# Product matmuls between the main matmuls of a two-layer graph kernel, one unit later

## The chip, the cores and the metric

The kernel runs on one core of one Trainium2 chip. The metric is the device time of one execution in microseconds (us). Engines: PE (TensorE) multiplies; PEld is PE's loading of stationary operands, which the trace records apart; DVE is VectorE, ACT ScalarE, POOL GpSimd, SP SyncE, which here issues DMAs.

## The reference

```python
def _L0_gnn_ref(h, adj, W_neigh, b_neigh, W_self, b_self):
    deg = jnp.sum(adj, axis=1, keepdims=True) + 1e-05
    adj_norm = adj / deg
    h_neigh = adj_norm @ h
    out = h_neigh @ W_neigh.T + b_neigh + h @ W_self.T + b_self
    return jax.nn.relu(out)

def _L1_gnn_ref(x, adj, W, b):
    rowsum = adj.sum(axis=1)
    d_inv_sqrt = jnp.where(rowsum > 0, rowsum ** (-0.5), 0.0)
    normalized_adj = d_inv_sqrt[:, None] * adj * d_inv_sqrt[None, :]
    support = normalized_adj @ x
    out = support @ W + b
    return jax.nn.relu(out)

x = _layernorm(x + _L0_gnn_ref(x, adj, ...), axis=-1)
x = _layernorm(x + _L1_gnn_ref(x, adj, ...), axis=-1)
```

x is 4096 x 256, adj 4096 x 4096, the weights are 256 x 256, all float32.

## The kernel before

**Tiles and units.** Each of the two layers goes through 8 blocks of 512 output rows. A block has 16 units (u = 0 to 15); a unit is one DMA of 128 x 1024 numbers of the transposed adj into a ring of 4 buffers `raw`. Every float32 operand is split in two parts: hi, the number rounded to the fp32r format (ACT, L256), and lo, the rest (DVE, L389). A product of two numbers is then three matmuls, hi x hi, lo x hi and hi x lo.

**Main matmuls (L675).** PE waits for `l_ready`, the lo of the unit, and issues 12 matmuls of 512 columns: 2 halves f of the features, 2 pieces q of 128 rows of adj, 3 passes each. They sum into `ps_main`, one of two PSUM buffers by the block's parity. The stationary operands are the features: `xs` in layer 0, `zs` (and the last part of `xs`) in layer 1. After a unit PE adds to `unit_done`; ACT's hi of the unit four later waits for that.

**The epilogue.** The sums of a block are finished while the next block runs: at unit 3 of their programs ACT and DVE split them into `st_hi` and `st_lo` (`stl_ready`), and PE multiplies them by the layer's weights, a product for each of the four tiles t of 128 rows: `product`, six matmuls of 256 columns in a row (L613), into `ps_epi[:, t, 0:256]`. `epilogue` places tile t behind the main matmuls of unit t + 1, and signals `tile_done`. In layer 0 eight matmuls of one column (L634) form the row sums behind unit 0, and the last tile waits until DVE has read these (`rs_copied`). DVE's program then has, in its unit 5 + t, `scale_product` (L419, waits for `tile_done`) ahead of the lo of that unit, `add_self` (L429) and `add_residual` (L436) behind it; ACT squares at its units 8 and 10 (L275), and norms and next features follow up to unit 15. DVE and ACT work through units ahead of PE, as far as the ring of four allows.

**The self product.** In layer 0 the product of x itself with `W_self` is formed in advance: `xt` is split into the same `st_hi` and `st_lo` at unit 9 (10 in the first block; `xt_unit`), after ACT has seen all four `tile_done`, and `prologue` places the six matmuls of tile t behind unit `xt_unit(b) + t` on PE, into `ps_epi[:, t, 256:512]`.

So there are 4 products in each of 15 epilogues and of 8 prologues, six matmuls each. The epilogue of the very last block has its own code (L693) and is left as it is. Every engine's program is in the order in which it is written; middle blocks run in a hardware loop.

Of the kernel before, what the change touches and what calls it, by code (L numbers as in the profile page):

```python
# [24 lines left out]
F = 256  # L25
P = 128
FH = F // P
# [3 lines left out]
TB = IB // P  # L31
UJ = 2
# [11 lines left out]
def build(nc, x_nat, xt_in, adj_in, wn_in, bn_in, ws_in, bs_in, w1_in, b1_in, out):  # L44
# [6 lines left out]
    with ctx:  # L51
        def sb(name, shape, dt=f32):
            return ctx.enter_context(nc.sbuf_tensor(name, shape, dt))

        def sem(name):
            return ctx.enter_context(nc.semaphore(name))
# [8 lines left out]
        acc = sb("acc", [P, 2, UW])  # L65
        st_hi = sb("st_hi", [P, FH, IB], f32r)
        st_lo = sb("st_lo", [P, FH, IB], f32r)
        xt = sb("xt_sb", [P, FH, IB])
        wn = sb("wn_sb", [P, 2, FH, F], f32r)
        ws = sb("ws_sb", [P, 2, FH, F], f32r)  # L70
# [6 lines left out]
        ones = sb("ones", [P, 1])  # L77
# [18 lines left out]
        ps_epi = ctx.enter_context(nc.psum_tensor("ps_epi", [P, TB, 2 * F], f32))  # L96
# [7 lines left out]
        ones_set = sem("ones_set")  # L104
        xh_ready, xl_ready = sem("xh_ready"), sem("xl_ready")
        wh_ready, wl_ready = sem("wh_ready"), sem("wl_ready")
        xth_ready, xtl_ready = sem("xth_ready"), sem("xtl_ready")
        h_ready, l_ready, acc_done = sem("h_ready"), sem("l_ready"), sem("acc_done")
        acc_folded = sem("acc_folded")
        unit_done = sem("unit_done")  # L110
        sth_ready, stl_ready = sem("sth_ready"), sem("stl_ready")
        rs_summed, rs_copied = sem("rs_summed"), sem("rs_copied")
        tile_done, tile_read = sem("tile_done"), sem("tile_read")
# [9 lines left out]
        def slot(u):  # L123
            return u % RING

        def is_last(e):

            return isinstance(e, int) and e == NB - 1

        def is_first(b):  # L130
            return isinstance(b, int) and b == 0

        def xt_unit(b):

            return 10 if is_first(b) else 9

        def x_stage(c):

            if c == 0:
                return acc[:, 1, :].rearrange("p (t f) -> p t f", t=XC)  # L140
            return (res, tt)[c % 2][:, :, :]
# [7 lines left out]
        def moving_weight(layer, part, k):  # L149
            if layer == 0:  # L150
                return wn[:, part, k, :]
            return (w1_lo if part else w1_hi)[:, k, :]

        def stationary(layer, part, jt, f):

            if layer == 0:
                return xs[:, jt, part, f * P:(f + 1) * P]
            src = zs[:, jt] if jt < ZOWN else xs[:, jt - ZOWN]
            return src[:, part, f * P:(f + 1) * P]

        def layers(eng, one_block, last_epilogue):


            for layer in range(2):
                one_block(layer, 0, 0, None if layer == 0 else (0, NB - 1))
                with eng.Fori(1, NB - 1, 2) as b:
                    one_block(layer, b, 1, (layer, b - 1))
                    one_block(layer, b + 1, 0, (layer, b))
                one_block(layer, NB - 1, 1, (layer, NB - 2))
            last_epilogue((1, NB - 1))  # L170
# [434 lines left out]

        @block.tensor
        def _(pe):
            def product(ps, rows, weight):

                passes = [(st_hi, 0), (st_hi, 1), (st_lo, 0)]  # L610
                for k in range(FH):
                    for q, (st, part) in enumerate(passes):
                        last = pe.matmul(ps, st[:, k, rows], weight(part, k),  # L613
                                         start=(k == 0 and q == 0), stop=(k == FH - 1 and q == 2))
                return last

            def prologue(b, u):

                t = u - xt_unit(b)
                if 0 <= t < TB:  # L620
                    if t == 0:
                        pe.wait_ge(wl_ready, 2)
                        pe.wait_ge(xtl_ready, b + 1)

                    product(ps_epi[:, t, F:2 * F], slice(t * P, (t + 1) * P), lambda part, k: ws[:, part, k, :])

            def epilogue(layer, e, parity, u):
                n = e + layer * NB
                if u == 0 and layer == 0:

                    pe.wait_ge(acc_folded, e + 1)
                    pe.wait_ge(ones_set, 1)
                    for t in range(TB):
                        last = pe.matmul(ps_epi[:, TB - 1, t:t + 1], acc[:, parity, t * P:(t + 1) * P],  # L634
                                         ones[:, :], start=True, stop=True)
                    last.then_inc(rs_summed, 1)
                if 1 <= u < 1 + TB:
                    t = u - 1
                    if t == 0:
                        pe.wait_ge(stl_ready, n + 1)  # L640
                    if t == TB - 1 and layer == 0:
                        pe.wait_ge(rs_copied, e + 1)

                    product(ps_epi[:, t, 0:F], slice(t * P, (t + 1) * P),
                            lambda part, k: moving_weight(layer, part, k)).then_inc(tile_done, 1)

            def one_block(layer, b, parity, epi):
                g0 = b * NU + layer * NB * NU
                ps = ps_main[parity]
                for u in range(NU):  # L650
                    if epi is None and u < WHOLE:

                        pe.wait_ge(x_first_full[u], 16)
                        pe.wait_ge(raw_full[slot(u)], 16)
                        for f, q in [(f, q) for f in range(FH) for q in range(UJ)]:
                            jt = u * UJ + q
                            last = pe.matmul(ps[:, f, :], x_stage(0)[:, jt, f * P:(f + 1) * P],  # L657
                                             raw[:, slot(u), q * IB:(q + 1) * IB], start=(jt == 0), stop=False)
                        last.then_inc(unit_done, 1)
                        continue  # L660
                    if epi is None and u % 2 == 0:
                        pe.wait_ge(xl_ready, u // 2 + 1)
                    if layer == 1 and epi[0] == 0:
                        pe.wait_ge(z_ready, UJ * (u + 1))
                    if layer == 1 and epi[0] == 1 and u == 0:
                        pe.wait_ge(wl_ready, 3)


                    pe.wait_ge(l_ready, g0 + (u + 1))
                    ends = layer == 1 and is_last(b) and u == NU - 1  # L670
                    for f, q in [(f, q) for f in range(FH) for q in range(UJ)]:
                        jt = u * UJ + q
                        cols = slice(q * IB, (q + 1) * IB)
                        for i, (part, mov) in enumerate(((0, hi), (0, lo), (1, hi))):
                            last = pe.matmul(ps[:, f, :], stationary(layer, part, jt, f), mov[:, slot(u), cols],  # L675
                                             start=(jt == 0 and i == 0), stop=(jt == JT - 1 and i == 2))
                        if ends and q == UJ - 1:
                            last.then_inc(half_done, 1)
                    if not ends:
                        last.then_inc(unit_done, 1)  # L680
                    if epi is not None:
                        epilogue(*epi, 1 - parity, u)
                    if layer == 0:
                        prologue(b, u)

            def last_epilogue(epi):
                n = 2 * NB - 1
                passes = [(st_hi, 0), (st_hi, 1), (st_lo, 0)]
                for k in range(FH):
                    pe.wait_ge(stl_ready, n + 1 + k)  # L690
                    for t in range(TB):
                        for q, (st, part) in enumerate(passes):
                            last = pe.matmul(ps_epi[:, t, 0:F], st[:, k, t * P:(t + 1) * P],  # L693
                                             moving_weight(1, part, k),
                                             start=(k == 0 and q == 0), stop=(k == FH - 1 and q == 2))
                        if k == FH - 1:
                            last.then_inc(tile_done, 1)

            layers(pe, one_block, last_epilogue)


# [33 lines left out]
```

## Time and profile before

| | us |
|---|---|
| median of 3 runs | 800.73 (800.4 to 802.11) |
| span of the profiled execution | 800.8 |
| PE busy | 782.1 (98%) |
| DVE busy | 577.4 (72%) |
| ACT busy | 386.9 (48%) |
| DMA of adj, share of 16 engines | 56.6% |

The profiled execution is within 0.1 us of the median. PE is busy all through the span; DVE is busier in layer 0 than in layer 1. Records of matmuls overlap (a matmul of 512 columns is recorded with 0.39 us while they start every 0.23 us), so the pace of PE is read from the starts, not from the busy time.

### The profile page before, as it was taken

The page shows a single profiled execution, that of the slowest core. Times are in us where ns is not written, and L with a number is a line of the kernel's source. Part 1 is how long each engine was busy: PE and PEld are TensorE (multiplying, and loading weights), DVE is VectorE, ACT ScalarE, POOL GpSimd, SP SyncE. Part 2 cuts the span into 40 slices and gives each one's busy share as a digit, 9 for nine tenths or more (in the row PEclk, how much of TensorE's full clock was granted, in tenths as well). Part 3 has the DMA queues.
Part 4 walks back from the last instruction along what each step waited for, and adds up shares of the span by engine and source line. Part 5 has one row for each costly group of instructions (what it writes and reads, how often), then busy time and mean ns, then how long its engine had stood idle before and what let it go on. Part 6 is the DMA issues. An engine that isn't in the chain of part 4 may idle for free.

```text
span 800.8 us, 11034 instructions
## 1 busy us (share of the span) xinstructions
PE 782.1 (98%) x3704; PEld 653.0 (82%) x3704; DVE 577.4 (72%) x868; ACT 386.9 (48%) x528; POOL 0.3 (0%) x6
## 2 busy tenths in 40 slices
PE   7899999999999999999999999999999999999995
PEld 4678888888888888888888888888888888888884
DVE  5799989899898998989966554555546455554643
ACT  3463745536446364454554545445444544545451
POOL 0000000000000000000000000000000000000000
PEclk9999999999999999999999999999999999999998
DMA  8767574755647556465565575746575574657540
GB/s 258 274 252 239 179 244 154 253 183 166 236 155 236 193 174 236 157 233 189 181 227 165 175 255 174 250 162 237 180 236 187 171 246 162 236 180 239 180 158 27
DMA packets 54459, 160.93 MB, mean 201 GB/s; under 512 B 5024, under 2 KB 18464, under 8 KB 54432
## 3 DMA queue, kind: packets, MB, share of 16 engines
q1 hardware_dynamic: 46224, 152.46, 56.6%
q10 hardware_dynamic: 8208, 8.13, 2.9%
q8 instruction: 15, 0.25, 0.1%
q14 instruction: 12, 0.10, 0.0%
HBM read 152.17 MB, written 8.39 MB: 201 GB/s over the span
## 4 chain that ended last, share of the span: by engine, by line
PE 94%; DMA 2%; DVE 2%; ACT 1%; issue 0%; SPq 0%
PE ps_main L675 84%; PE ps_epi L613 8%; DMA raw<-adj_t 2%; PE ps_main L657 1%; PE ps_epi L634 1%; DMA tt<-x_nat 1%; DVE lo L389 0%; DVE acc L565 0%; ACT hi L256 0%; PE ps_epi L693 0%; DVE tt L436 0%; DVE stats L585 0%; DVE tt L419 0%; DVE xs L389 0%; ACT tt L359 0%
## 5 line engine op out<-in xcount | busy, mean ns | idle before, releaser
L256 ACT ACTIVATE hi<-raw 128x1024 fp32r<-128x1024 f32 x254 | 269.4, 1061 | 352.8 <-PE ps_main L675 327.8
L389 DVE TENSOR_TENSOR lo<-raw,hi 128x1024 fp32r<-128x1024 f32 x254 | 310.4, 1222 | 145.3 <-ACT hi L256 145.2
L675 PE MATMUL ps_main<-hi,xs 128*128 128x512 f32 x1136 | 366.3, 392 | 4.3 <-DVE lo L389 4.3
L675 PE MATMUL ps_main<-hi,zs 128*128 128x512 f32 x896 | 283.0, 390 | 0.0
L675 PEld LDWEIGHTS ps_main<-hi,xs 128*128 128x128 f32 x1136 | 214.2, 189 | 49.3 <-DVE lo L389 3.6
L675 PE MATMUL ps_main<-lo,xs 128*128 128x512 f32 x568 | 222.4, 392 | 0.0
L675 PEld LDWEIGHTS ps_main<-hi,zs 128*128 128x128 f32 x896 | 168.3, 188 | 34.3
L675 PE MATMUL ps_main<-lo,zs 128*128 128x512 f32 x448 | 174.7, 390 | 0.0
L565 DVE TENSOR_TENSOR acc<-acc,raw 128x1024 f32<-128x1024 f32 x112 | 136.3, 1217 | 0.0
L675 PEld LDWEIGHTS ps_main<-lo,xs 128*128 128x128 f32 x568 | 107.3, 189 | 20.0 <-issue 0.2
L675 PEld LDWEIGHTS ps_main<-lo,zs 128*128 128x128 f32 x448 | 84.2, 188 | 16.3
L419 DVE SCALAR_TENSOR_TENSOR tt<-ps_epi,d_cur,bias 128x256 f32<-128x256 f32 x32 | 15.4, 483 | 39.2 <-PE ps_epi L613 38.5
L389 DVE TENSOR_TENSOR st_lo<-ps_main,st_hi 128x1024 fp32r<-128x1024 f32 (+1 forms) x17 | 19.8, 1162 | 21.6 <-ACT st_hi L256 21.6
L281 ACT ACTIVATE tt<-tt,nmr,inv_root 128x256 f32<-128x256 f32 x60 | 32.5, 588 | 4.3 <-DVE nmr L473 4.3
L256 ACT ACTIVATE st_hi<-ps_main 128x1024 fp32r<-128x1024 f32 (+1 forms) x17 | 16.6, 978 | 33.3 <-PE ps_main L675 33.3
L275 ACT ACTIVATE ps_epi<-tt,nmean 128x256 f32<-128x256 f32 x60 | 27.5, 459 | 0.0
L436 DVE SCALAR_TENSOR_TENSOR tt<-tt,res 128x256 f32<-128x256 f32 x64 | 26.8, 419 | 0.2
L613 PE MATMUL ps_epi<-ws_sb,st_hi 128*128 128x256 f32 x128 | 24.2, 282 | 0.0
L613 PE MATMUL ps_epi<-wn_sb,st_hi 128*128 128x256 f32 x128 | 24.2, 282 | 0.0
L613 PEld LDWEIGHTS ps_epi<-ws_sb,st_hi 128*128 128x128 f32 x128 | 22.0, 190 | 2.5
L613 PEld LDWEIGHTS ps_epi<-wn_sb,st_hi 128*128 128x128 f32 x128 | 22.0, 190 | 2.5
L613 PE MATMUL ps_epi<-xs,st_hi 128*128 128x256 f32 x112 | 21.2, 282 | 0.0
(74 smaller groups left out, 322.7 us busy)
## 6 DMA issues: line engine op xcount, KB each, us to landing
raw<-adj_t SPq DMA_DIRECT2D x256, 512.0 KB, 3.3
res<-x_nat SPq DMA_DIRECT2D x11, 512.0 KB, 6.4
xt_sb<-xt SPq DMA_DIRECT2D x8, 512.0 KB, 5.0
x_scratch<-tt ACTq DMA_DIRECT2D x8, 512.0 KB, 6.2
res<-x_scratch SPq DMA_DIRECT2D x8, 512.0 KB, 6.0
out<-tt ACTq DMA_DIRECT2D x7, 512.0 KB, 6.4
tt<-x_nat SPq DMA_DIRECT2D x4, 512.0 KB, 6.4
acc<-x_nat SPq DMA_DIRECT2D x2, 256.0 KB, 3.6
```

The costliest lines, as they stand in the source:

```text
L256: return act.activation(dst, src, ACT.Copy)
L275: act.activation(ps_epi[:, t, 0:F], tt[:, t, :], ACT.Square, bias=nmean[:, t:t + 1], accum_out=squares[:, t:t + 1]).then_inc(squares_ready, 1)
L281: act.activation(tt[:, t, :], tt[:, t, :], ACT.Identity, bias=nmr[:, t:t + 1], scale=rstd[:, t:t + 1]).then_inc(x1_ready, 1)
L389: return dve.tensor_tensor(dst, src, hi_part.bitcast(f32), ALU.subtract)
L419: ins = dve.scalar_tensor_tensor(out=tt[:, t, :], in0=ps_epi[:, t, 0:F], scalar=(rdeg, d_cur)[layer][:, t:t + 1], in1=(bias0, bias1)[layer ...
L436: link(dve.scalar_tensor_tensor(out=tt[:, t, :], in0=tt[:, t, :], scalar=0.0, in1=res[:, t, :], op0=ALU.max, op1=ALU.add, accum_out=sums[: ...
L565: dve.tensor_tensor(a, a, raw[:, slot(u), :], ALU.add).then_inc(acc_done, 1)
L613: last = pe.matmul(ps, st[:, k, rows], weight(part, k), start=(k == 0 and q == 0), stop=(k == FH - 1 and q == 2))
L634: last = pe.matmul(ps_epi[:, TB - 1, t:t + 1], acc[:, parity, t * P:(t + 1) * P], ones[:, :], start=True, stop=True)
L657: last = pe.matmul(ps[:, f, :], x_stage(0)[:, jt, f * P:(f + 1) * P], raw[:, slot(u), q * IB:(q + 1) * IB], start=(jt == 0), stop=False)
L675: last = pe.matmul(ps[:, f, :], stationary(layer, part, jt, f), mov[:, slot(u), cols], start=(jt == 0 and i == 0), stop=(jt == JT - 1 and ...
```

## The change

Each product is cut into its six matmuls, `product_step`. In a unit with a product, the step m // 2 is issued ahead of main matmul m for m = 1, 3, 5, 7, 9, 11. The row of six that stood behind unit u stands thus inside unit u + 1: `epilogue` takes tile u - 2, `prologue` tile u - xt_unit(b) - 1. The row sums stay behind unit 0, in a function of their own. Waits and signals go with their matmuls.

```diff
+            def product_step(step, ps, rows, weight):
+                k, q = divmod(step, len(passes))
+                st, part = passes[q]
+                return pe.matmul(ps, st[:, k, rows], weight(part, k), start=(step == 0), stop=(step == STEPS - 1))
...
+            def self_tile(b, u):
+                return u - xt_unit(b) - 1
...
-                if 1 <= u < 1 + TB:
-                    t = u - 1
-                    if t == 0:
-                        pe.wait_ge(stl_ready, n + 1)
-                    if t == TB - 1 and layer == 0:
-                        pe.wait_ge(rs_copied, e + 1)
-                    product(ps_epi[:, t, 0:F], slice(t * P, (t + 1) * P),
-                            lambda part, k: moving_weight(layer, part, k)).then_inc(tile_done, 1)
+                t = u - 2
+                if (t, step) == (0, 0):
+                    pe.wait_ge(stl_ready, n + 1)
+                if (t, step) == (TB - 1, 0) and layer == 0:
+                    pe.wait_ge(rs_copied, e + 1)
+                last = product_step(step, ps_epi[:, t, 0:F], slice(t * P, (t + 1) * P),
+                                    lambda part, k: moving_weight(layer, part, k))
+                if step == STEPS - 1:
+                    last.then_inc(tile_done, 1)
...
                         for i, (part, mov) in enumerate(((0, hi), (0, lo), (1, hi))):
+                            m = fq * 3 + i
+                            if m % 2 and epi is not None and 2 <= u < 2 + TB:
+                                epilogue(*epi, u, m // 2)
+                            if m % 2 and layer == 0 and 0 <= self_tile(b, u) < TB:
+                                prologue(b, u, m // 2)
...
-                    if epi is not None:
-                        epilogue(*epi, 1 - parity, u)
-                    if layer == 0:
-                        prologue(b, u)
+                    if epi is not None and epi[0] == 0 and u == 0:
+                        row_sums(epi[1], 1 - parity)
```

The orders of ACT, DVE and SP are the same before and after. On PE, in the first block, the end of unit 10 and the start of unit 11 before, with the first self product (`ws_sb` is W_self) between the units:

```order
L675 MATMUL ps_main<-lo,xs 128x512
L675 MATMUL ps_main<-hi,xs 128x512
L613 MATMUL ps_epi<-ws_sb,st_hi 128x256 [waits xtl_ready,wl_ready]
L613 MATMUL ps_epi<-ws_sb,st_hi 128x256
L613 MATMUL ps_epi<-ws_sb,st_lo 128x256
L613 MATMUL ps_epi<-ws_sb,st_hi 128x256 x2
L613 MATMUL ps_epi<-ws_sb,st_lo 128x256
L675 MATMUL ps_main<-hi,xs 128x512 [waits l_ready]
L675 MATMUL ps_main<-lo,xs 128x512
```

The self product has moved behind the wait for the lo of unit 11, and into the unit. The same place after the change (L682 are the main matmuls, L615 the products):

```order
L682 MATMUL ps_main<-lo,xs 128x512
L682 MATMUL ps_main<-hi,xs 128x512
L682 MATMUL ps_main<-hi,xs 128x512 [waits l_ready]
L615 MATMUL ps_epi<-ws_sb,st_hi 128x256 [waits xtl_ready,wl_ready]
L682 MATMUL ps_main<-lo,xs 128x512
L682 MATMUL ps_main<-hi,xs 128x512
L615 MATMUL ps_epi<-ws_sb,st_hi 128x256
L682 MATMUL ps_main<-hi,xs 128x512
L682 MATMUL ps_main<-lo,xs 128x512
L615 MATMUL ps_epi<-ws_sb,st_lo 128x256
L682 MATMUL ps_main<-hi,xs 128x512 x2
```

In the loop of layer 1, on PE: the end of unit 1 and the start of unit 2 before, with the product of tile 0 (the moving operand, W of layer 1, lies in `xs`) between them:

```order
L675 MATMUL ps_main<-hi,zs 128x512
L640 REGISTER_ALU
L613 MATMUL ps_epi<-xs,st_hi 128x256 [waits stl_ready]
L613 MATMUL ps_epi<-xs,st_hi 128x256
L613 MATMUL ps_epi<-xs,st_lo 128x256
L613 MATMUL ps_epi<-xs,st_hi 128x256 x2
L613 MATMUL ps_epi<-xs,st_lo 128x256
L669 REGISTER_ALU
L675 MATMUL ps_main<-hi,zs 128x512 [waits l_ready]
```

The product's wait for `stl_ready` has moved from the end of unit 1 behind the first main matmul of unit 2, and the six stand singly there:

```order
L682 MATMUL ps_main<-hi,zs 128x512 [waits l_ready]
L641 REGISTER_ALU
L615 MATMUL ps_epi<-xs,st_hi 128x256 [waits stl_ready]
L682 MATMUL ps_main<-lo,zs 128x512
L682 MATMUL ps_main<-hi,zs 128x512
L615 MATMUL ps_epi<-xs,st_hi 128x256
L682 MATMUL ps_main<-hi,zs 128x512
L682 MATMUL ps_main<-lo,zs 128x512
L615 MATMUL ps_epi<-xs,st_lo 128x256
```

No two products follow each other any more; two main matmuls stand between them, also from one unit to the next.

## Rows read from the trace of the kernel before

**Rows 1.** The page: busy time by engine; granted clock; the chain's shares.

```profile
PE 782.1 (98%) x3704; PEld 653.0 (82%) x3704; DVE 577.4 (72%) x868; ACT 386.9 (48%) x528; POOL 0.3 (0%) x6
...
PEclk9999999999999999999999999999999999999998
...
PE 94%; DMA 2%; DVE 2%; ACT 1%; issue 0%; SPq 0%
PE ps_main L675 84%; PE ps_epi L613 8%; DMA raw<-adj_t 2%; PE ps_main L657 1%; PE ps_epi L634 1%; DMA tt<-x_nat 1%; DVE lo L389 0%; DVE acc L565 0%; ACT hi L256 0%; PE ps_epi L693 0%; DVE tt L436 0%; DVE stats L585 0%; DVE tt L419 0%; DVE xs L389 0%; ACT tt L359 0%
```

**Rows 2.** Waits of PE: waiter <- releaser: us in total, times, longest.

```profile
PE ps_main L675 <- DVE lo L389: 4.3, 3, 3.1
```

**Rows 3.** The chain in order of time: start us, us, what.

```profile
278.03 0.71 PE ps_epi L613 x6
278.74 2.75 PE ps_main L675 x12
281.49 0.71 PE ps_epi L613 x6
282.20 13.63 PE ps_main L675 x60
...
433.38 35.39 PE ps_main L675 x156
```

**Rows 4.** Timeline of PE in a middle block: start us, us, engine, line, what.

```profile
277.87 0.40 PE L613 MATMUL ps_epi<-wn_sb,st_hi 128*128 128x256 f32 x2
278.10 0.28 PE L613 MATMUL ps_epi<-wn_sb,st_lo 128*128 128x256 f32 x1
...
278.58 0.40 PE L675 MATMUL ps_main<-hi,xs 128*128 128x512 f32 x1
278.81 0.40 PE L675 MATMUL ps_main<-lo,xs 128*128 128x512 f32 x1
279.05 0.62 PE L675 MATMUL ps_main<-hi,xs 128*128 128x512 f32 x2
...
279.74 0.62 PE L675 MATMUL ps_main<-hi,xs 128*128 128x512 f32 x2
...
280.42 0.62 PE L675 MATMUL ps_main<-hi,xs 128*128 128x512 f32 x2
```

**Rows 5.** Line 613: count, ns of one min/median/max, first and last start.

```profile
L613 PE MATMUL ps_epi<-ws_sb,st_hi x128: 277/283/283, 46.4 to 407.3; 128*128 128x256 f32 x128
...
L613 PE MATMUL ps_epi<-wn_sb,st_hi x128: 277/283/283, 69.4 to 433.0; 128*128 128x256 f32 x128
...
L613 PE MATMUL ps_epi<-xs,st_hi x112: 277/283/283, 468.6 to 758.3; 128*128 128x256 f32 x112
```

**Rows 6.** Timeline of PE, the row sums (a record of one is 0.25).

```profile
267.28 0.95 PE L634 MATMUL ps_epi<-ones,acc 128*128 128x1 f32 x8
```

**Rows 7.** Timeline of PE in the first block, units 10 and 11.

```profile
43.62 0.47 PE L675 MATMUL ps_main<-hi,xs 128*128 128x512 f32 x1 [0.94 <-DVE lo L389]
43.93 0.39 PE L675 MATMUL ps_main<-lo,xs 128*128 128x512 f32 x1
...
46.42 0.40 PE L613 MATMUL ps_epi<-ws_sb,st_hi 128*128 128x256 f32 x2
...
47.13 0.40 PE L675 MATMUL ps_main<-hi,xs 128*128 128x512 f32 x1
```

**Rows 8.** Timeline of DVE, the lo of units 10, 11 and 12.

```profile
42.24 1.23 DVE L389 TENSOR_TENSOR lo<-raw,hi 128x1024 fp32r<-128x1024 f32 x1 [0.67 <-ACT hi L256]
...
45.66 1.22 DVE L389 TENSOR_TENSOR lo<-raw,hi 128x1024 fp32r<-128x1024 f32 x1
...
49.06 1.22 DVE L389 TENSOR_TENSOR lo<-raw,hi 128x1024 fp32r<-128x1024 f32 x1
```

**Rows 9.** Timeline of DVE, the lo of units 8 and 9, middle block.

```profile
282.64 1.22 DVE L389 TENSOR_TENSOR lo<-raw,hi 128x1024 fp32r<-128x1024 f32 x1
...
286.08 1.23 DVE L389 TENSOR_TENSOR lo<-raw,hi 128x1024 fp32r<-128x1024 f32 x1 [0.41 <-ACT hi L256]
```

**Rows 10.** Timeline of ACT there: the split of xt and the next hi.

```profile
283.48 1.04 ACT L256 ACTIVATE st_hi<-xt_sb 128x1024 fp32r<-128x1024 f32 x1
284.99 1.06 ACT L256 ACTIVATE hi<-raw 128x1024 fp32r<-128x1024 f32 x1 [0.47 <-PE ps_main L675]
```

More of the change, by code:

```diff
@@ L607, in _ @@
         def _(pe):
[L608 to L620, printed above, removed]
-                    if t == 0:
-                        pe.wait_ge(wl_ready, 2)
-                        pe.wait_ge(xtl_ready, b + 1)
-                    product(ps_epi[:, t, F:2 * F], slice(t * P, (t + 1) * P), lambda part, k: ws[:, part, k, :])
@@ L627, in epilogue @@
-            def epilogue(layer, e, parity, u):
-                n = e + layer * NB
[L629 to L636, printed above, removed]
-                if 1 <= u < 1 + TB:
-                    t = u - 1
-                    if t == 0:
-                        pe.wait_ge(stl_ready, n + 1)
-                    if t == TB - 1 and layer == 0:
-                        pe.wait_ge(rs_copied, e + 1)
-                    product(ps_epi[:, t, 0:F], slice(t * P, (t + 1) * P),
-                            lambda part, k: moving_weight(layer, part, k)).then_inc(tile_done, 1)
+            passes = [(st_hi, 0), (st_hi, 1), (st_lo, 0)]
@@ new lines, in _, with prologue @@
+            STEPS = FH * len(passes)
+            def product_step(step, ps, rows, weight):
[4 more added lines that the diff above has]
+                return u - xt_unit(b) - 1
+            def prologue(b, u, step):
+                t = self_tile(b, u)
+                if (t, step) == (0, 0):
+                    pe.wait_ge(wl_ready, 2)
+                    pe.wait_ge(xtl_ready, b + 1)
+                product_step(step, ps_epi[:, t, F:2 * F], slice(t * P, (t + 1) * P), lambda part, k: ws[:, part, k, :])
@@ new lines, in row_sums, with epilogue @@
+            def row_sums(e, parity):
+                pe.wait_ge(acc_folded, e + 1)
+                pe.wait_ge(ones_set, 1)
+                for t in range(TB):
+                    last = pe.matmul(ps_epi[:, TB - 1, t:t + 1], acc[:, parity, t * P:(t + 1) * P],
+                                     ones[:, :], start=True, stop=True)
+                last.then_inc(rs_summed, 1)
+            def epilogue(layer, e, u, step):
+                n = e + layer * NB
+                t = u - 2
+                if (t, step) == (0, 0):
+                    pe.wait_ge(stl_ready, n + 1)
[5 more added lines that the diff above has]
+                    last.then_inc(tile_done, 1)
@@ L670, in one_block @@
                     ends = layer == 1 and is_last(b) and u == NU - 1
-                    for f, q in [(f, q) for f in range(FH) for q in range(UJ)]:
+                    for fq, (f, q) in enumerate([(f, q) for f in range(FH) for q in range(UJ)]):
                         jt = u * UJ + q
@@ L680, in one_block @@
                         last.then_inc(unit_done, 1)
-                    if epi is not None:
-                        epilogue(*epi, 1 - parity, u)
-                    if layer == 0:
-                        prologue(b, u)
+                    if epi is not None and epi[0] == 0 and u == 0:
+                        row_sums(epi[1], 1 - parity)
             def last_epilogue(epi):
                 n = 2 * NB - 1
-                passes = [(st_hi, 0), (st_hi, 1), (st_lo, 0)]
                 for k in range(FH):
```

## The prediction

> **What bounds the kernel now.** I read the page first: TensorE (PE) is busy 98% of the span at the full granted clock (2.4 GHz), and 94% of the chain that ended last is PE, 84% on the main matmuls of L675 and 8% on the product matmuls of L613 [rows 1]. Then the waits: a main matmul waited for VectorE only 3 times, 4.3 us in all [rows 2], and these lie in the first 44 us. So after the start only two things can move the time: the pace at which PE takes matmuls, and a new wait. The busy share cannot show the pace, since matmul records overlap; the reader is to look at the starts in the PE timeline and at the lengths of pieces in the chain.
>
> There the paces are these. Main matmuls undisturbed: 156 in 35.39 us, 0.2269 us each [rows 3]. A unit with a product: 12 main matmuls 2.75 us, the six product matmuls 0.71 us, a period of 3.46 us from 278.03 to 281.49 [rows 3]. Inside it [rows 4]: the first two of six products take 0.23 us together (277.87 to 278.10), the last four 0.48 us (278.10 to 278.58), 0.120 each. The record of the first is 277 ns long against a median of 283 [rows 5], so I read the first at 0.113 to 0.114, the others at 0.119 to 0.120. Behind the six, five main matmuls are slow: 278.58 to 279.74 is 1.16 us, 0.232 each; from 279.74 to 280.42 three take 0.68 us, 0.227 each, as undisturbed. The six and the recovery behind them are thus dearer than an undisturbed pace: 12 x 0.2269 + 6 x 0.1133 (half a main matmul) = 3.402 us against 3.46, so 0.058 us a unit. There are (128 + 128 + 112) products with st_hi [rows 5], four in each unit, hence 368 / 4 = 92 such units: 5.3 us in all. That is the whole stake on PE's pace.
>
> **The change, part by part.** Nothing is added or removed: same matmuls, same weight loads; the order on ACT, DVE and SP stays as it was, and so do their DMAs.
>
> *The interleaving.* Each product now stands behind two main matmuls. What is a lone product worth? Not shown in this trace: in all 92 units six stand in a row. Bounds: the first of a row takes 0.113 and is preceded by a main matmul as every one will be; the later ones take 0.120. The main matmul behind it: 0.2269 if undisturbed, 0.232 as behind the row. A common account fits both sizes: at 2.4 GHz 512 columns are 0.2133 us and 256 are 0.1067; the undisturbed main matmul is 0.0135 dearer than its columns, and the later products are too (0.120 - 0.1067 = 0.013). If a pair of load and matmul costs its columns plus 0.0135 in whatever order, a unit costs 12 x 0.2133 + 6 x 0.1067 + 18 x 0.0135 = 3.443 us. Today's 3.46 is 0.017 above that, which I put to the crowding in the row of six. I take that value, because it explains the 0.120 and the 0.2269 by one number; the cheap first product then is a cost that comes later. 92 x 0.017 = **1.6 us saved**. Both ends: 92 x 0.058 = 5.3 us saved if the lone product takes 0.113 and leaves no trace; and, if each lone product takes 0.113 but slows two main matmuls as the first two behind the row (278.58 to 279.05, 0.47 against 0.454, so 0.016), 6 x 0.016 = 0.096 in place of 0.058: 0.038 x 92 = 3.5 us lost.
>
> The Trainium skill ("TensorE: Matmul & The Clock Gate", section "LDWEIGHTS (loading the stationary operand)") puts the load of 128 columns at columns over 1.2 GHz, 107 ns. By this figure a 256-column matmul just covers the next load and no order is dearer than another for that reason; the trace is near to it, for 8 one-column matmuls, each with a load, take 0.95 - 0.25 = 0.70 us for seven steps, 0.10 each [rows 6].
>
> *One unit later, at the start.* In the first block the products of st_hi from xt stood behind unit 10 and now begin in unit 11. Behind unit 10 they filled a gap: PE finished the main matmuls at 46.42, ran six products, and began unit 11 at 47.13 [rows 7]. Unit 11 needs the lo of that unit, which DVE writes from 45.66 to 46.88 [rows 8]. At unit 10 the lo ended at 42.24 + 1.23 = 43.47 and PE began at 43.62, 0.15 later, and its first matmul took 0.31 us instead of 0.23 [rows 7, 8]. So unit 11 will begin at 46.88 + 0.15 = 47.03, with PE idle for 0.61 us, 0.08 us more in the first matmul, and the six products still to do: **0.7 us lost**. Nothing gives it back: the lo of unit 12 ends at 49.06 + 1.22 = 50.28 [rows 8], before PE would want it in either order (50.59 today, 47.03 + 0.08 + 3.44 = 50.55 then), so it made up for nothing before and makes up for nothing now. This is a wait that the products covered, and it happens once.
>
> *One unit later, in the blocks.* The sums of a unit do not move: its units end where main matmuls and six products ended before. But tile_done of a tile comes at the last main matmul of the unit that followed, 2.75 - 0.23 = 2.5 us later. DVE stands in order, and its scale_product of unit 5 holds the lo behind it. Who waits for that: PE, at the start of each unit. Cover: the lo of unit 8 ends at 282.64 + 1.22 = 283.86 [rows 9] and PE begins unit 8 at 282.20 + 3 x 2.72 = 290.36 [rows 3], 6.5 us later; the lo of unit 9 ends at 287.31 [rows 9] against 293.1, 5.8 us. Less 2.5 us, at least 3.3 us are left; the price is nothing, and if the cover were gone each lost microsecond would stand in 8 or 15 blocks. On ACT the split of xt (283.48) waits for tile_done of all four tiles and stands ahead of the hi of unit 9 (284.99) [rows 10]; it moves by about 1.3 us, the hi by about 0.8, inside the same cover. The waits for st_lo and for xt's lo on PE come later than before, so they gain room. Cost nothing.
>
> **Sum.** 800.8 (the profiled execution's own span, 0.1 us from the median of 800.73) - 1.6 + 0.7 = **799.9 us**.
>
> **The rivals.**
> 1. *All of the crowding goes.* Lone products at 0.113, main matmuls at 0.2269: 800.8 - 5.3 + 0.7 = 796.2. For it: the first of each six, the only one behind a main matmul, is the cheap one in the timeline [rows 4, 5]. Against: what follows a cheap one is dearer, every time. The load rule of "TensorE: Matmul & The Clock Gate" in the Trainium skill, named above, leads the same way: with 107 ns for a load nothing would hold a lone product back.
> 2. *The cost is merely spread.* Each product brings its 0.058 / 6 = 0.010 us wherever it stands, partly on itself, partly on the main matmul behind it: 800.8 + 0.7 = 801.5. For it: the extra falls partly on the six and partly on the five behind, as a debt would.
> 3. *Slower: two main matmuls slow behind every product.* PE gets ahead on instructions only while it works slowly; a product uses one up fast. Six products and five slow main matmuls, 11 pairs, take 0.71 + 1.16 = 1.87 us until the pace is back: PE's queue is refilled at up to one pair in 0.170 us. Behind a lone product one main matmul is enough if a pair arrives in less than (0.113 + 0.232) / 2 = 0.172 us. That is the point from which it decides, and it is close. Beyond it the second main matmul is slow as well: 800.8 + 3.5 + 0.7 = 805.0, and half of that pace loss, 803.2, if the second one is hit every other time.
> 4. *A stall.* The delayed tile_done eats DVE's lead. The lead above speaks against it. If PE came to wait 1 us in each of the 15 blocks with an epilogue, it would be 815.
>
> **How the numbers follow.** Forecast 0.42, rival 1 0.20, rival 2 0.15, rival 3 0.18, rival 4 and anything else 0.05. A measurement of this kernel tells 0.2%, 1.6 us, from no change. Rival 1 is faster; the forecast at 0.9 us is within it, with perhaps a quarter of its weight beyond since a slow main matmul of 0.232 with a product of 0.113 would give 3.433 a unit, 92 x 0.027 = 2.5 saved, 799.0: faster 0.32. Rival 2 and the rest of the forecast, and a little of rival 3: same 0.47. Rival 3 and 4: slower 0.21. The range holds forecast, rivals 1 and 2 and the milder half of rival 3: 795.9 to 803.0.
>
> **What would show it.** In the PE timeline of the changed kernel, pairs of main matmuls and a product: a cycle of 0.574 us (3.443 / 6) for the forecast, 0.567 for rival 1, 0.577 for rival 2, 0.583 for rival 3. In the chain, a new wait of a main matmul for lo near 46.4, 0.6 us idle; if it is missing the start was misread. Among the waits, DVE's L419 for PE should grow by up to 2.5 us for each first tile, and PE should have no wait for DVE after 50 us; one there would be rival 4. A time under 796 or over 803 would mean that lone products have a price outside both ends.

## The result and the profile after

The changed kernel takes 807.5 us (median of 5 runs, 806.7 to 808.04) against 800.73; the ratio is 1.0079 with a 95% interval of 1.0067 to 1.0091. It is slower by 6.8 us by the medians, by 6.3 us (5.4 to 7.3) by the ratio, where 0.9 us less was forecast, and outside the range. The profiled execution took 807.3 us, with a span of 805.5. Every execution here whose span is on record takes 1.7 to 2.0 us longer than its span, so the one profiled before, with a span of 800.8, took about 802.6 us by estimate. That it was within 0.1 us of the median, as the table before says, compares a span with a time; the base of the forecast's sum is right all the same, since the median of the times is 800.73. Up to unit 10 of the first block the two kernels run the same program, and yet that unit begins at 43.62 us in the profile before [rows 7] and at 41.90 in the one after. So the pace is compared over blocks in the middle, not over spans.

The page of the changed kernel shows nothing amiss: the busy share and the clock read as in [rows 1].

```profile
PE 787.3 (98%) x3704; PEld 653.0 (81%) x3704; DVE 575.6 (71%) x868; ACT 387.1 (48%) x528; POOL 0.3 (0%) x6
...
PEclk9999999999999999999999999999999999999998
```

The chain in order of time (start us, us, what) gives the period of a block of layer 1, from the end of one group of four products to the end of the next, first in the changed kernel:

```profile
485.55 33.14 PE ps_main L682 x146
...
532.28 2.76 PE ps_main L682 x12
```

532.28 - 485.55 = 46.73 us. In the kernel before it is 46.48 (479.86 to 526.34):

```profile
479.86 35.39 PE ps_main L675 x156
...
526.34 3.88 PE ps_main L675 x17
```

So four units with a product cost 0.25 us more, 0.063 each. In layer 0 a block has eight such units. The row sums of two blocks follow each other there after 319.52 - 268.62 = 50.90 us in the changed kernel, and after 317.83 - 267.44 = 50.39 before:

```profile
268.62 0.79 PE ps_epi L633 x8
...
319.52 0.79 PE ps_epi L633 x8
```

```profile
267.44 0.79 PE ps_epi L634 x8
...
317.83 0.79 PE ps_epi L634 x8
```

0.51 us for eight is 0.064 each, the same again. 92 x 0.063 = 5.8 us. The timeline of PE shows it (changed kernel, layer 1, third of the four units); main matmuls (L682) and products (L615) start at:

```profile
479.40 0.28 PE L615 MATMUL ps_epi<-xs,st_hi 128*128 128x256 f32 x1
479.52 0.39 PE L682 MATMUL ps_main<-hi,zs 128*128 128x512 f32 x1
479.75 0.40 PE L682 MATMUL ps_main<-lo,zs 128*128 128x512 f32 x1
479.99 0.28 PE L615 MATMUL ps_epi<-xs,st_lo 128*128 128x256 f32 x1
...
481.75 0.28 PE L615 MATMUL ps_epi<-xs,st_lo 128*128 128x256 f32 x1
```

Four cycles take 481.75 - 479.40 = 2.35 us, 0.587 for two main matmuls and a product. Forecast were 0.574; rival 3 had 0.583. No matmul of the cycle runs at its undisturbed pace: the product takes 0.12 where [rows 4] have 0.113 for a first one, and the two main matmuls together 0.47 (479.52 to 479.99). Undisturbed, a main matmul takes 0.2267 us: `wide_between`, below, has 12 matmuls of 512 columns in 2.72 us. The prediction's 0.2269 was a mean over 156 of them that took in the dearer ones behind a row.

The other part lies at the start. PE's timeline there:

```profile
44.51 0.39 PE L682 MATMUL ps_main<-hi,xs 128*128 128x512 f32 x1
45.21 0.50 PE L682 MATMUL ps_main<-hi,xs 128*128 128x512 f32 x1 [0.31 <-DVE lo L389]
45.55 0.28 PE L615 MATMUL ps_epi<-ws_sb,st_hi 128*128 128x256 f32 x1
```

The new wait of unit 11 for its lo is there, 44.51 to 45.21 where 0.23 would do: 0.47 us, and the first matmul takes 0.34 in place of 0.23. That is 0.6 of the 0.7 us forecast. And 5.8 + 0.6 = 6.4 us, inside the interval of the ratio.

DVE waits longer for the products, and the profile lists no wait of PE after the first 50 us. Such a list can miss a short wait, but the blocks of layer 0 also follow each other evenly (row sums at 217.72, 268.62 and 319.52). Waits of DVE (us in total, times, longest), before and after:

```profile
DVE tt L419 <- PE ps_epi L613: 42.6, 32, 1.8
```

```profile
DVE tt L419 <- PE ps_epi L615: 82.4, 39, 4.4
```

### The profile page after: what moved, and what is told of

It reads as the page before. It is cut to its first block, busy times and chain, and to the rows that moved or that the text cites. A ratio compares the mean times of both kernels' runs of the same rounds, so it can differ in the third digit from the quotient of the medians.

```text
span 805.5 us, 11034 instructions
## 1 busy us (share of the span) xinstructions
PE 787.3 (98%) x3704; PEld 653.0 (81%) x3704; DVE 575.6 (71%) x868; ACT 387.1 (48%) x528; POOL 0.3 (0%) x6
## 4 chain that ended last, share of the span: by engine, by line
PE 94%; DVE 2%; DMA 2%; ACT 1%; issue 0%; SPq 0%
PE ps_main L682 84%; PE ps_epi L615 8%; DMA raw<-adj_t 1%; PE ps_main L659 1%; PE ps_epi L633 1%; DMA tt<-x_nat 1%; DVE lo L389 1%; DVE acc L565 0%; ACT hi L256 0%; PE ps_epi L697 0%; DVE st_lo L389 0%; DVE tt L436 0%; DVE stats L585 0%; DVE tt L419 0%; DVE xs L389 0%
## 5 line engine op out<-in xcount | busy, mean ns | idle before, releaser
L682 PE MATMUL ps_main<-hi,xs 128*128 128x512 f32 x1136 | 372.6, 393 | 3.9 <-DVE lo L389 3.9
L682 PE MATMUL ps_main<-hi,zs 128*128 128x512 f32 x896 | 286.6, 391 | 0.0
L682 PEld LDWEIGHTS ps_main<-hi,xs 128*128 128x128 f32 x1136 | 205.6, 188 | 43.9 <-DVE lo L389 3.6
L682 PE MATMUL ps_main<-lo,xs 128*128 128x512 f32 x568 | 222.5, 392 | 0.0
L682 PEld LDWEIGHTS ps_main<-hi,zs 128*128 128x128 f32 x896 | 164.1, 188 | 31.2
L682 PE MATMUL ps_main<-lo,zs 128*128 128x512 f32 x448 | 175.0, 391 | 0.0
L682 PEld LDWEIGHTS ps_main<-lo,xs 128*128 128x128 f32 x568 | 106.7, 188 | 18.3 <-issue 0.2
L682 PEld LDWEIGHTS ps_main<-lo,zs 128*128 128x128 f32 x448 | 84.1, 188 | 15.4
L615 PE MATMUL ps_epi<-wn_sb,st_hi 128*128 128x256 f32 x128 | 36.3, 284 | 0.0
L615 PE MATMUL ps_epi<-ws_sb,st_hi 128*128 128x256 f32 x128 | 36.3, 284 | 0.0
L419 DVE SCALAR_TENSOR_TENSOR tt<-ps_epi,rdeg,bias 128x256 f32<-128x256 f32 x32 | 15.5, 484 | 25.6 <-PE ps_epi L615 24.7
L615 PE MATMUL ps_epi<-xs,st_hi 128*128 128x256 f32 x112 | 31.8, 284 | 0.0
L615 PEld LDWEIGHTS ps_epi<-wn_sb,st_hi 128*128 128x128 f32 x128 | 24.0, 187 | 5.4
L615 PEld LDWEIGHTS ps_epi<-ws_sb,st_hi 128*128 128x128 f32 x128 | 24.0, 187 | 5.3
```

Of the source, the lines that this page charges most:

```text
L419: ins = dve.scalar_tensor_tensor(out=tt[:, t, :], in0=ps_epi[:, t, 0:F], scalar=(rdeg, d_cur)[layer][:, t:t + 1], in1=(bias0, bias1)[layer ...
L615: return pe.matmul(ps, st[:, k, rows], weight(part, k), start=(step == 0), stop=(step == STEPS - 1))
```

## The experiments

**Lateness or interleaving?** Two kernels each do one half of the change. `row_later` has the six products in a row, in the later unit. Its edit to the changed kernel:

```diff
+            PLACES = {1: (0, 1, 2, 3, 4, 5)}
...
-                            m = fq * 3 + i
-                            if m % 2 and epi is not None and 2 <= u < 2 + TB:
-                                epilogue(*epi, u, m // 2)
-                            if m % 2 and layer == 0 and 0 <= self_tile(b, u) < TB:
-                                prologue(b, u, m // 2)
+                            for step in PLACES.get(fq * 3 + i, ()):
+                                if epi is not None and 2 <= u < 2 + TB:
+                                    epilogue(*epi, u, step)
+                                if layer == 0 and 0 <= self_tile(b, u) < TB:
+                                    prologue(b, u, step)
```

> The six product matmuls stand in a row again, but in the later unit (ahead of its second main matmul), so that only the lateness of the change is left. Theory A (PE has a slow state, in which every pair of load and matmul is about 6.7 ns dearer whatever its width; a product brings PE into it and a stretch of main matmuls alone brings it out; ten such pairs a unit with a row of six, all 18 with lone products): the unit with a product takes 3.460 us as before, and only the wait at the start is lost: 800.7 + 0.7 = 801.4. Theory B (the lateness itself is what costs, through tile_done and DVE): near 807.

Measured: 801.2 us against 800.54 of the kernel before on the same chip, ratio 1.0007 (0.9997 to 1.0016). The unit with a product is back at 2.75 + 0.71 us, and a block of layer 1 at 477.60 to 524.08, 46.48. In layer 0 the row sums of two blocks are at 264.79 and 315.18, 50.39 apart, as before.

```profile
477.60 35.39 PE ps_main L683 x156
...
524.08 5.92 PE ps_main L683 x26
```

At the start the wait for unit 11's lo is there too:

```profile
43.06 0.39 PE L683 MATMUL ps_main<-hi,xs 128*128 128x512 f32 x1
43.79 0.50 PE L683 MATMUL ps_main<-hi,xs 128*128 128x512 f32 x1 [0.35 <-DVE lo L389]
44.13 0.40 PE L616 MATMUL ps_epi<-ws_sb,st_hi 128*128 128x256 f32 x2
```

0.73 us in place of 0.23, and 0.34 in place of 0.23 behind it: 0.6 us. The median moved by 0.7, though its interval holds no change too. Lateness costs what the start shows, once, and nothing in the blocks.

`between_not_later` does the other half (the first block's self products stay in rows):

```diff
+            PLACES = {1: (0,), 3: (1,), 5: (2,), 7: (3,), 9: (4,), 11: (5,)}
...
-                return u - xt_unit(b) - 1
+                return u - xt_unit(b)
...
-                t = u - 2
+                t = u - 1
...
+                    if layer == 0 and is_first(b) and 0 <= self_tile(b, u) < TB:
+                        for step in range(STEPS):
+                            prologue(b, u, step)
```

> The products stand between the main matmuls but not a unit later: epilogue tile t in unit t + 1, self tile t in unit xt_unit + t; only the first block's self products stay in a row behind their units as before, so that the start is untouched. 88 of 92 units are interleaved. Theory A: 88 x 0.063 = 5.5 us above the kernel before, 806.3, with a cycle of 0.587 us for two main matmuls and a product. Theory B: near 800.7.

Measured: 806.38 us, ratio 1.0075 (1.0059 to 1.0092), 5.8 us over the kernel before. A block of layer 1 takes 528.13 - 481.40 = 46.73 us, as in the changed kernel:

```profile
481.40 33.14 PE ps_main L683 x146
...
528.13 2.08 PE ps_main L683 x9
```

The interleaving alone makes the loss in the blocks. Once, in the second block, a product waited for `st_lo`, about 0.4 us, since there it is needed earlier than in either other kernel.

**What makes a product between main matmuls dear?** At this point theory A took every pair of load and matmul to be 6.7 ns dearer for a while after a product, theory C a fixed price for each change of kind. `rows3` is `row_later` with two rows of three products, PLACES = {5: (0, 1, 2), 11: (3, 4, 5)}.

> Two rows of three products a unit, each behind five or six main matmuls, one unit later. Theory A (slow pairs counted): a row of three slows its second and third product and some of the six main matmuls behind it; if PE recovers within the six, 2 x (2 + 3) = 10 to 2 x (2 + 5) = 14 slow pairs, a unit of 3.47 to 3.49 us, 801.9 to 804. If it never recovers, all 18, 3.52 us and 807. Theory C (each change from products to main matmuls costs a fixed 12 ns and each product 8, which fits a row of six and lone products alike): 2 x 12.4 + 6 x 7.9 = 72 ns above 3.400, 3.472 us, 802.5.

Measured: 802.97 us, ratio 1.0032 (1.002 to 1.0044). A block of layer 1 (chain, from the end of the eight rows of three to the next) has

```profile
481.01 34.03 PE ps_main L683 x150
...
527.57 2.52 PE ps_main L683 x11
```

46.56 us, 0.08 over the kernel before, so a unit of 3.48 us: 0.020 us for one row more. In its timeline a row of three is followed by the same slow main matmuls as a row of six: from 515.23 to 516.39 there are five in 1.16 us, 0.232 each.

```profile
514.88 0.40 PE L616 MATMUL ps_epi<-xs,st_hi 128*128 128x256 f32 x2
515.11 0.28 PE L616 MATMUL ps_epi<-xs,st_lo 128*128 128x256 f32 x1
515.23 0.63 PE L683 MATMUL ps_main<-hi,zs 128*128 128x512 f32 x2
515.70 0.39 PE L683 MATMUL ps_main<-lo,zs 128*128 128x512 f32 x1
515.92 0.62 PE L683 MATMUL ps_main<-hi,zs 128*128 128x512 f32 x2
516.39 0.39 PE L683 MATMUL ps_main<-lo,zs 128*128 128x512 f32 x1
```

That speaks against a debt in proportion to the products. The next two leave products out; their outputs are others, and what is read is the pace of PE in one profiled execution of each. `half_apart4` issues steps 0, 3 and 5 ahead of main matmuls 3, 7 and 11; `lone` only step 5, ahead of main matmul 5.

> Leaves out three of the six matmuls of each product; the other three stand alone, each with four main matmuls ahead of it. Undisturbed a unit would be 12 x 0.2267 + 3 x 0.1133 = 3.060 us. Theory A, if four main matmuls let PE recover: the product at 0.113 and one to three slow main matmuls, 10 to 15 ns a product, 3.09 to 3.10 us. Theory A, if they do not: five slow pairs a product, 33 ns each, 3.16 us. Theory C: 20 ns a product, 3.12 us.

Measured: a product and four main matmuls take 542.66 - 540.58 = 2.08 us for two such cycles (timeline below), 1.04 each, against 4 x 0.2267 + 0.1133 = 1.020: 20 ns a product by these two, and 22 by the six cycles of the chain from 538.66 to 544.91. The four main matmuls between two products take 0.92 to 0.93 us in that chain, against 0.907. This is near theory C, and neither form of A.

```profile
540.58 0.28 PE L616 MATMUL ps_epi<-xs,st_lo 128*128 128x256 f32 x1
...
542.66 0.28 PE L616 MATMUL ps_epi<-xs,st_hi 128*128 128x256 f32 x1
```

> Leaves out five of the six matmuls of each product: one narrow matmul a unit, with 12 main matmuls between two. It measures the price of one by itself. Theory A' (recovery has a fixed length of five main matmuls, as behind rows of three and six): 27 ns each above 0.1133, a product unit of 2.720 + 0.113 + 0.027 = 2.861 us. The refill theory of the prediction (recovery in proportion to the products): 4 to 7 ns each, 2.838 to 2.841 us.

Measured, in the chain of `lone`: the period of a unit is 526.04 - 523.18 = 2.86 us, that is 0.140 for one lone product above 12 x 0.2267 = 2.720. That is 0.027 over 0.1133, as much as behind a row of six.

```profile
523.18 2.75 PE ps_main L683 x12
525.92 0.12 PE ps_epi L616
526.04 2.75 PE ps_main L683 x12
```

The other end is a row of 24. `row24` has all four products of an epilogue behind unit 1, and all self products behind unit 12, unit 10 in the first block:

```diff
+                    for t, step in [(t, step) for t in range(TB) for step in range(STEPS)]:
+                        if epi is not None and u == 1:
+                            epilogue(*epi, t, step)
+                        if layer == 0 and u == (10 if is_first(b) else 12):
+                            prologue(b, t, step)
```

> All four products of an epilogue in one row of 24 behind unit 1, all four self products in one row behind unit 12 (unit 10 in the first block). Theory A': one recovery of 27 ns and 23 x 6.6 ns for 24 products, 179 ns in place of 4 x 60 = 242; 23 rows, 1.45 us below the kernel before: 799.1. If a long row drains PE's queue of instructions, as the row sums seem to (a first main matmul of 0.324 behind them and nine slow ones), up to 0.12 more a row, 2.8 us: 801.9.

Measured: 800.28 us (median of 11) against 801.28 of the kernel before (15), ratio 0.9987 (0.9977 to 0.9998). It is the fastest of the kernels that form all products, by 0.13%; the expectation had 1.45 us less than before, and 1.0 was measured. A block of layer 1 takes 516.07 - 469.65 = 46.42 us, 0.06 less than before, for three returns fewer:

```profile
466.77 2.87 PE ps_epi L615 x24
469.65 43.55 PE ps_main L671 x192
...
516.07 43.55 PE ps_main L671 x192
```

24 products take 2.87 us, 0.120 each to the last, and a slow stretch of the same size follows (43.55 - 192 x 0.2267 = 0.02). PE was fed a pair of load and matmul every 0.120 us for 2.87 us: its instructions are not short. Once, in the second block, it waited for `rs_copied` (0.4 us), which is about what the whole falls short of the expectation.

**Width or place?** From here on the kernels compute other outputs, and each has one profiled execution. `wide_between` is the changed kernel with epilogue products of 512 columns, `w384_between` with 384; only the slices differ:

```diff
+                whole = (wn[:, 0], wn[:, 1]) if layer == 0 else (w1_hi, w1_lo)
+                last = product_step(step, ps_epi[:, t, :], slice(t * P, (t + 1) * P),
+                                    lambda part, k: whole[part].rearrange("p k f -> p (k f)"))
```

> As the changed kernel, but each matmul of the epilogue's products is as wide as a main matmul: 512 columns (both halves of the weights side by side) into the whole ps_epi tile, so the outputs are others. The self products in layer 0 keep 256 columns; layer 1 is read. Theory A' (what slows PE is a matmul narrower than its neighbours; behind one, alone or the last of a row, five main matmuls are slow by 27 ns together, unless the next product cuts that short): no narrow matmul, so no slow state, and the cycle of two main matmuls and a product is 3 x 0.2267 = 0.680 us. Theory D (the change of PSUM tile between ps_main and ps_epi costs): about 0.700 us, 20 ns more.

Measured, PE in layer 1: from 541.86 to 544.58, four cycles, 2.72 us, 0.680 each. Nothing is lost: the change of tile and of operands costs nothing. It is the width.

```profile
541.86 0.39 PE L616 MATMUL ps_epi<-xs,st_lo 128*128 128x512 f32 x1
...
544.58 0.39 PE L616 MATMUL ps_epi<-xs,st_hi 128*128 128x512 f32 x1
```

> As the one before, with 384 columns a product matmul in the epilogues. Undisturbed the cycle would be 2 x 0.2267 + 0.170 = 0.623 us. Theory A' with any width below 512: 0.64 us, 20 ns more. Theory E (only a matmul that is shorter than the load of the next stationary operand slows PE; loads start every 0.11 to 0.12 us in a row of products, and 384 columns take 0.17): 0.623, nothing lost.

Measured, PE in layer 1: from 530.75 to 532.67, three cycles, 1.92 us, 0.640 each. The expectation's undisturbed 0.623 took three quarters of 0.2267 for the product; by columns and 0.0133, as the others are counted below, it is 2 x 0.2267 + 0.173 = 0.627. Narrower by a quarter already slows PE, by 13 ns a cycle, and theory E falls.

```profile
530.75 0.34 PE L616 MATMUL ps_epi<-xs,st_lo 128*128 128x384 f32 x1
...
532.67 0.34 PE L616 MATMUL ps_epi<-xs,st_lo 128*128 128x384 f32 x1
```

The last three are `lone` with another width in the epilogues.

> Leaves out five of the six matmuls of each product; the one left in the epilogues has 384 columns, with 12 main matmuls to the next. Theory F (the recovery grows with the columns that the matmul lacks to 512; 256 lacking gave 27 ns): 128 lacking, about 13 ns over two or three main matmuls. Theory G (any narrow matmul costs the same recovery): 27 ns over five.

> The same with 480 columns. Theory F: 32 lacking, 3 ns or nothing. Theory G: 27 ns over five main matmuls.

> The same with one step as two matmuls of 128 columns in a row, in the epilogues. Theory F: 384 lacking in the last of them, about 40 ns over seven or more main matmuls (the one-column row sums, 511 lacking, are followed by nine slow ones, 47 ns beside a first one of 0.324). Theory G: 27 ns over five.

In the chain of `lone384` and then of `lone480` a unit takes 528.46 - 525.54 = 2.92 and 528.52 - 525.54 = 2.98 us; in that of `two128` 528.45 - 525.50 = 2.95:

```profile
525.54 2.75 PE ps_main L684 x12
...
528.46 2.75 PE ps_main L684 x12
```

```profile
525.54 2.77 PE ps_main L684 x12
...
528.52 2.77 PE ps_main L684 x12
```

```profile
525.50 2.78 PE ps_main L684 x12
...
528.45 2.78 PE ps_main L684 x12
```

Above 2.720 that is 0.200 for 384 columns, 0.260 for 480 and, over three units of the chain, 0.233 for two of 128. With columns plus 0.0133 they would be 0.173, 0.213 and 0.133. The extra is 0.027, 0.047 and 0.10, with 0.020 for 256 and nothing for 512. Both theories fall: 384 alone would fit theory G, but 480, the widest of the narrow ones, is the dearest of the three, so the extra neither grows with the columns that lack nor is it one price.

The number of slow main matmuls grows with the width. Behind 256 columns five are slow (`lone`: 523.01 to 524.17 in PE's timeline). Behind 384 and behind 480, in the timelines of `lone384` and then of `lone480`, there are six in 526.77 - 525.38 = 1.39 us and nine in 527.46 - 525.38 = 2.08 us, 0.231 each, and the rest is undisturbed:

```profile
525.38 0.62 PE L684 MATMUL ps_main<-hi,zs 128*128 128x512 f32 x2
...
526.77 0.62 PE L684 MATMUL ps_main<-hi,zs 128*128 128x512 f32 x2
```

```profile
525.38 0.63 PE L684 MATMUL ps_main<-hi,zs 128*128 128x512 f32 x2
...
527.46 0.62 PE L684 MATMUL ps_main<-hi,zs 128*128 128x512 f32 x2
```

The 0.10 of two matmuls of 128 is of another kind. In the timeline of `two128` they start at 525.16 and 525.22, and the first main matmul at 525.34: the second of them takes 0.12 where its columns plus 0.0133 are 0.067. The row sums (L634) of the kernel before have the like: three matmuls of one column, each with a load, in 267.75 - 267.41 = 0.34 us, 0.11 each.

```profile
267.41 0.81 PE L634 MATMUL ps_epi<-ones,acc 128*128 128x1 f32 x6
```

```profile
267.75 0.47 PE L634 MATMUL ps_epi<-ones,acc 128*128 128x1 f32 x3
```

So about half of the 0.10 looks like a least time of a matmul with its load in a row, 0.11 us at 1 and at 128 columns alike; the rest is one main matmul behind the pair that takes 0.28 (525.34 to 525.62). `two128` therefore says little on the return from the wider ones.

## Why the prediction was wrong

**The bound, the stake, the count.** Right. PE's pace sets the time outside the start, a unit with a product is 0.058 us over the undisturbed pace (0.060 with 0.2267), there are 92.

**The interleaving: the step that failed.** The step is "If a pair of load and matmul costs its columns plus 0.0135 in whatever order, a unit costs ... 3.443 us. Today's 3.46 is 0.017 above that, which I put to the crowding in the row of six". The first half holds for the sizes, and not for "whatever order": rows of 3, 6 and 24 take n x 0.120, and 512-column products in any place 0.2267, but a change of width costs. The second half put the 0.017 in the wrong place. It does not come from the row; rows of any length pay it once, when PE returns to 512 columns: 27 ns over five main matmuls, less the 7 by which the first product was cheap, 20 ns. One lone product, rows of 3, 6 and 24 gave 0.140, 0.380, 0.740 and 2.89 us a row (the period less the main matmuls at 0.2267), each within 0.01 of n x 0.120 + 0.020. The change makes six returns of one. Cut short by the next product each costs 0.587 - 2 x 0.2267 - 0.120 = 0.014 us: 6 x 0.014 = 0.084 in place of 0.020, which is the 0.063 measured. So I took the trace's clear sign, five slow main matmuls behind every row, for the last part of a price that the row had run up, where it was the price of leaving the row, and the change multiplies leaving by six.

**The bounds.** The lower end of the interleaving lost 3.5 us, the measurement 5.8. It had a lone product at 0.113 with two slow main matmuls; where products come every two main matmuls the product itself also takes 0.12. No row of the trace before showed a product behind a slow main matmul, and both ends gave it the cheap value. The Trainium skill ("TensorE: Matmul & The Clock Gate", section "LDWEIGHTS (loading the stationary operand)") puts the load of 128 columns at 107 ns. The trace is near to it, with 0.11 us for a one-column matmul with its load, shown above. (The prediction read 0.10 there: it averaged over seven steps, of which the first two take 0.13 us together, 267.28 [rows 6] to 267.41.) By this load nothing would hold a lone product of 256 or 384 columns back, and the runs of both disagree: 27 ns are lost behind each.

**The start.** Right in place and nearly in size, 0.6 of 0.7 us, in both kernels that are late.

**The blocks.** Right: DVE's waits for products grew from 42.6 to 82.4 us in all, the longest from 1.8 to 4.4, 2.6 where up to 2.5 was forecast, and no wait of PE came of it. `row_later` shows no loss there.

**The rivals.** Rival 3 was nearest, with 805.0 us and 0.583 a cycle. Its mechanism fell, however: `row24` feeds a pair in 0.120 us without end, so PE's queue is not refilled at 0.170, and the recovery behind a row does not grow with the row. So its being nearest is luck. Rival 1 fell, and rival 2, that the cost is spread by product, too: its price goes by rows. Rival 4 did not come.

## What to carry to other kernels

On PE, narrow matmuls belong in long rows of their own, and not between wide ones: what costs is each return from 256 to 512 columns (20 ns here, 14 where the next product comes after two main matmuls), so count the returns that a new order makes. Where the trace shows a slow stretch behind a row, find out whether it belongs to the row or to its end before moving its members apart; one kernel with a row of another length tells it. And before work is moved to a later place, look for the wait that it happened to cover.

## What the runs showed of the hardware

Behind a matmul of 256 to 480 columns, the next ones of 512 columns take about 0.232 us in place of 0.2267, 2% more, though the granted clock is at full speed (a mean of 0.994 to 0.997 of 2.4 GHz) and the instructions arrive in time: five of them are slow behind 256, six behind 384, nine behind 480, where they are not cut short. The price of a lone matmul, above its columns at 2.4 GHz and 13 ns, is 20 ns at 256 columns, 27 at 384, 47 at 480, and none at 512. Two of 128 cost 0.10 us, about half of it because the second of the pair takes 0.12, as a one-column matmul with its load takes 0.11.

What in PE makes this stays open. Neither the tile, nor the operands, nor a shortage of instructions is the cause: 512 columns in the same places cost nothing, and 24 products run evenly in a row. That 480 is dearest of the three rather speaks for a matter of phase between loads and matmuls than for one of amount, but this is argued, not shown.
